# Head shifts of a unit turned in one group, local values by tokens, and query and key parts laid out by head

## What is computed

```python
k_c = k_pad.reshape(B, H, nb, G * D) @ Wck      # 32 blocks of 16 keys, compressed
out_c = softmax(where(c_ok, q @ k_c / scale, NEG)) @ v_c
_, top_idx = jax.lax.top_k(logits_c, 4)         # the 4 best blocks of each token
out_s = softmax over the keys of those blocks, where key <= token
wmask = (abs(pos[:, None] - pos[None, :]) <= 32) & (pos[:, None] >= pos[None, :])
out_l = softmax(where(wmask, q @ k / scale, NEG)) @ v
out = gates[..., 0:1] * merge(out_c) + gates[..., 1:2] * merge(out_s) + gates[..., 2:3] * merge(out_l)
return out @ Wo
```

## Time and profile before

| | |
|---|---|
| median of 3 runs | 1507.11 us (1507.01 to 1509.83) |
| the profiled execution | 1507.87 us, its span in the trace 1506.1 us |
| mean granted TensorE clock | 0.979 of full speed |
| TensorE busy | 1420.1 us, 94% of the span |
| VectorE / ScalarE / GpSimd busy | 1187.8 / 928.4 / 919.1 us |
| DMA | 113.74 MB, 76 GB/s over the span |

### The profile page before, as it was taken

The page is one execution under the profiler, slowest core; times in us unless marked ns, Lnnn a source line. Parts: engine busy times, 40 slices in busy tenths (PEclk is TensorE's granted clock), DMA queues, the critical chain, the costliest instruction groups (busy, mean ns, idle before and its releaser), DMA issues. The chain is left out here.

```text
span 1506.1 us, 43877 instructions
## 1 busy us (share of the span) xinstructions
PE 1420.1 (94%) x14960; PEld 1044.1 (69%) x14960; DVE 1187.8 (79%) x4544; ACT 928.4 (62%) x1684; POOL 919.1 (61%) x845
## 2 busy tenths in 40 slices
PE   6899679999999999999999999999999999999978
PEld 4566447777777777777777777777777777777657
DVE  5444288888888888888888888898888888888812
ACT  3766336666666666666666666666666666666641
POOL 4655356666666666666666666666666666666620
PEclk8999879999999999999999999999999999999989
DMA  6556942221111122222111122212222222222027
GB/s 186 205 183 211 274 73 53 52 51 45 47 45 47 50 51 51 51 51 50 47 46 46 47 50 49 48 48 51 51 51 51 51 51 51 65 51 53 9 95 234
DMA packets 217147, 113.74 MB, mean 76 GB/s; under 512 B 128872, under 2 KB 211224, under 8 KB 217112
## 3 DMA queue, kind: packets, MB, share of 16 engines
q1 hardware_dynamic: 216304, 112.88, 27.3%
q10 hardware_dynamic: 808, 0.42, 0.2%
HBM read 73.08 MB, written 40.16 MB: 75 GB/s over the span
## 5 line engine op out<-in xcount | busy, mean ns | idle before, releaser
L1150 POOL TENSOR_TENSOR sumxy<-xy 128x1024 f32<-128x1024 f32 x128 | 240.7, 1901 | 0.0
L1393 DVE TENSOR_REDUCE bmax<-q_bank 128x32 f32<-128x512 f32 (+3 forms) x512 | 219.9, 481 | 16.5 <-PE q_bank L1633 15.4
L1240 ACT ACTIVATE pts<-k_bank 128x512 f32<-128x512 f32 (+2 forms) x384 | 177.4, 490 | 42.0 <-PE k_bank L1668 41.2
L1494 DVE SCALAR_TENSOR_TENSOR mw<-sumxy,c,ex 128x1024 f32<-128x1024 f32 x128 | 176.0, 1394 | 1.5 <-issue 0.8
L1633 PE MATMUL q_bank<-ko,qo 96*128 96x512 bf16 (+3 forms) x512 | 142.9, 306 | 24.6 <-DVE bmax L1393 22.6
L1116 POOL TENSOR_TENSOR pad<-pad 128x1 f32<-128x1 f32 x32 | 6.2, 193 | 256.4 <-DVE top L1412 256.4
L1615 PE MATMUL f_bank<-xt,wfu 128*128 128x128 f32 x1024 | 162.3, 281 | 0.0
L1174 POOL TENSOR_TENSOR cw<-cw,mw 128x1024 f32<-128x1024 f32 x64 | 150.8, 2356 | 6.6 <-ACT mw L1264 1.6
L1615 PE MATMUL f_bank<-xt,wfg 128*128 128x128 f32 x1024 | 150.3, 279 | 0.0
L1615 PEld LDWEIGHTS f_bank<-xt,wfu 128*128 128x128 f32 x1024 | 139.4, 191 | 11.5
L1264 ACT ACTIVATE mw<-mw,erec 128x1024 f32<-128x1024 f32 x128 | 145.7, 1139 | 0.0
(11 more groups left out here) (211 smaller groups left out, 3340.1 us busy)
## 6 DMA issues: line engine op xcount, KB each, us to landing
qo<-s_qs SPq DMA_DIRECT2D x192, 64.0 KB, 2.2
ko<-s_ks SPq DMA_DIRECT2D x186, 64.0 KB, 2.2
s_qs<-parts SPq DMA_DIRECT2D x8, 768.0 KB, 4.7
s_ks<-parts SPq DMA_DIRECT2D x8, 768.0 KB, 6.3
s_v<-vo SPq DMA_DIRECT2D x8, 544.0 KB, 3.0
vv<-s_v SPq DMA_DIRECT2D x32, 136.0 KB, 2.3
vw<-s_v SPq DMA_DIRECT2D x64, 68.0 KB, 2.5
xin<-in_L_attn_x_dram SPq DMA_DIRECT2D x8, 512.0 KB, 6.9
```

The lines of the kernel that those rows point to most:

```text
L1150: done("sum_done", g_.tensor_tensor(sumxy[:, h, :, :], xy[:, 0, h, 0:XK, None].broadcast_to([P, XK, KEYS]), xy[:, 1, h, None, :].broadcast ...
L1240: last = s.activation(pts[:, h, OFFS[j]:OFFS[j] + n], bank[:, 0:n], ACT.Exp)
L1393: last = v.tensor_reduce(bmax[:, i, h, 0:n], Q.bank(job)[:, o:o + n * BLK].rearrange("p (n j) -> p n j", j=BLK), AX.X, ALU.max)
L1494: done("mw_done", v.scalar_tensor_tensor(mw[:, h, :], sumxy[:, h, :, :].rearrange("p a b -> p (a b)"), c8[:, h, 7:8], ex[:, h % 2, :], ALU ...
```

## The change

1. `qo` and `ko` are laid out by head. The six parts lie in three pairs, and the pair that would lie in a head's own quarter (rows 32h to 32h + 31 for head h) lies in the last quarter instead. The own quarter of head h holds the shifts of that head; the one of head 3 is the last. Until the shifts are there it holds zeros, loaded from a small DRAM tensor `s_zero` that the setup fills. So `queries` and `window` use all 128 rows. The loads become 20 DMAs for queries (4 of zeros) and 16 for keys, 36 in place of 12.
2. The shifts of the four heads are turned by one group of 4 products of 128 columns of weights, the first of the step, and ScalarE copies the four quarters one after the other ahead of its tanh (job a, first of ring K).
3. The local values are made by tokens: the exponentials are the weights, the values stream, and the result needs no turning back. The 64 products come in two halves on either side of `mlp_down(t, 3)`; a signal vl_half keeps the second from starting before the first is done. VectorE reads the bank directly; job tl, a copy on ScalarE and four transposes go.
4. `expert_sum` stands ahead of `key_marks`.
5. `yr` of batch 0 is loaded during the unit stage, and batch 1 waits for its `ar` alone before its transposes.
6. In the unit stage's lead, the block rows of `ko` come by 4 DMAs from ScalarE's queue in place of a copy on GpSimd. Some signals are merged into one with a count (strike_pc, xy_cand, e8_nmax).

```diff
-            SP3 = 96
+            PARTS = ((0, 0), (2, 0)), ((0, 1), (0, 2)), ((1, 0), (1, 1))
...
-            k_jobs = ["pcT", "co", "a0"]
+            k_jobs = ["a", "pcT", "co"]
             for h in range(HG):
-                k_jobs += [f"s{h}0", f"s{h}1", f"s{h}2"] + [f"a{h + 1}"] * (h < HG - 1) + [("pl0", "pl1", "vl", "tl")[h]]
-            k_jobs += ["vs", "ts"]
+                k_jobs += [f"s{h}0", f"s{h}1", f"s{h}2"] + [f"pl{h}"] * (h < 2)
+            k_jobs += ["vl", "vs", "ts"]
...
+            def part_rows(to, src, which, half):
+
+                for i, pair in enumerate(PARTS):
+                    lots = [(3, i, i + 1)] + [(i, h0, h1) for h0, h1 in ((0, i), (i + 1, HG)) if h0 < h1]
+                    for quad, h0, h1 in lots:
+                        for n in range(2):
+                            o = 32 * quad + D * n
+                            yield to[o:o + D, half, h0:h1, :], src[pair[n][which]][:, h0:h1, :]
...
-                    pairs = [(to[D * n:D * n + D, half, :, :], src[r])
-                             for to, src, parts in ((qo, q, Q_ROWS), (ko, k, K_ROWS))[:2 if keys else 1] for n, r in enumerate(parts)]
-                    send(pairs, parts_in[half], N_PARTS if keys else N_PARTS // 2)
+                    pairs = [(qo[32 * h:32 * h + 32, half, h, :], s_zero) for h in range(HG)]
+                    pairs += part_rows(qo, q, 0, half)
+                    if keys:
+                        pairs += part_rows(ko, k, 1, half)
+                    send(pairs, parts_in[half], N_PARTS if keys else N_QUERIES)
...
+                sp.dma_start(yr0[:, :, :], s_y[0:G].rearrange("i p c -> p i c")).then_inc(batch_in[0], 16)
...
-                for n, r in enumerate(K_ROWS):
-                    act.dma_start(ko[D * n:D * n + D, 0, :, :], k_first[r]).then_inc(parts_in[0], 16)
+                for h in range(HG):
+                    act.dma_start(ko[32 * h:32 * h + 32, :, h, :],
+                                  onehot[96:128, None, :].broadcast_to([32, 2, T])).then_inc(key_blocks, 16)
+                for dst, src in part_rows(ko, k_first, 1, 0):
+                    act.dma_start(dst, src).then_inc(parts_in[0], 16)
...
+                def head_shifts(t):
+
+                    K.wait_full(act, t, "a")
+                    for h in range(HG):
+                        rows = slice(32 * h, 32 * h + 32)
+                        last = s.activation(qo[rows, t.half, h, :], K.bank("a")[rows, :], ACT.Copy)
+                    K.released("a", last)
...
                 def step(t):
                     n = None if t.tail else t.next()
+                    head_shifts(t)
                     tanh(t, "w0", sw[:, 0:512], "tw_done")
...
+                    expert_sum(t)
+                    if n:
                         key_marks(n)
...
-                def local_values(t):
+                def local_values(t, r):
 
                     bank = K.bank("vl")
-                    for g in range(T // 32):
-                        for h in range(HG):
-                            rows, k = slice(64 * (h // 2), 64 * (h // 2) + 64), h % 2
-                            last = mm(bank[32 * h:32 * h + VW, 32 * g:32 * g + 32], vw[rows, t.half, g, VW * k:VW * k + VW],
-                                      pT[rows, k, 32 * g:32 * g + 32], start=True, stop=True, skip_group_check=True)
-                    K.filled("vl", last)
+                    rows = slice(64 * r, 64 * r + 64)
+                    for k in range(2):
+                        for g in range(T // 32):
+                            i, q = divmod(g, 4)
+                            o = VW * (HG * i + 2 * r + k)
+                            last = mm(bank[32 * q:32 * q + 32, o:o + VW], pT[rows, k, 32 * g:32 * g + 32],
+                                      vw[rows, t.half, g, VW * k:VW * k + VW], start=True, stop=True, skip_group_check=True)
+                    if r == 0:
+                        done("vl_half", last)
+                    else:
+                        K.filled("vl", last)
```

More of the change, by code:

```diff
@@ L273, in build @@
             b4 = sb("b4", [96, 2, 2, P], BF16)
+            zeros = sb("zeros", [32, T], BF16)
             bank = [ps(f"sbank{i}", [P, 512]) for i in range(4)]
@@ L299, in _ @@
                     sp.dma_start(dst, src).then_inc(to, 16)
-                sp.wait_ge(proj_in, 3 * 16)
+                sp.wait_ge(zeroed, 1)
+                sp.dma_start(s_zero, zeros[:, :]).then_inc(proj_in, 16)
+                sp.wait_ge(proj_in, 4 * 16)
             @block.gpsimd
@@ L311, in _ @@
                 g.memset(b1[:, :, :, :], 0.0).then_inc(cleared, 1)
+                g.memset(zeros[:, :], 0.0).then_inc(zeroed, 1)
                 for k, m in enumerate((ident, identb)):
@@ L879, in build @@
         projecting.close()
+        sb, _, _ = make(outer)
+        yr0 = sb("yr0", [P, TT, C])
         inner = ExitStack()
@@ L1338, in step @@
                     shifts_and_blocks(t)
-                    openings(t)
+                    tanh(t, "g0", hidden(0), "th_done")
                     share(t, 2)
@@ L1632, in queries @@
                         n = P * (i + 1)
-                        last = mm(bank[:, o:o + n], qo[0:SP3, t.half, h, P * i:P * i + P], ko[0:SP3, t.half, h, 0:n],
+                        last = mm(bank[:, o:o + n], qo[:, t.half, h, P * i:P * i + P], ko[:, t.half, h, 0:n],
                                   start=True, stop=(i > 0))
@@ L1651, in window @@
                                 o = 64 * (TT * h2 + i)
-                                k_ = (ko[0:SP3, t.half, h, s0 - 32:s0 + 32] if s0 else
-                                      ko[0:SP3, t.half, h, 0:32][:, None, :].broadcast_to([SP3, 2, 32]))
-                                last = mm(bank[32 * q:32 * q + 32, o:o + 64], qo[0:SP3, t.half, h, s0:s0 + 32], k_,
+                                k_ = (ko[:, t.half, h, s0 - 32:s0 + 32] if s0 else
+                                      ko[:, t.half, h, 0:32][:, None, :].broadcast_to([P, 2, 32]))
+                                last = mm(bank[32 * q:32 * q + 32, o:o + 64], qo[:, t.half, h, s0:s0 + 32], k_,
                                           start=False, stop=True, skip_group_check=True)
@@ L1659, in keys_rows @@
                 def keys_rows(t, h, part):
-                    if part == 0:
-                        K.wait_read(pe, t, f"a{h}")
+                    if (h, part) == (0, 0):
+                        K.wait_read(pe, t, "a")
                     job = f"s{h}{part}"
@@ L1763, in mlp_down @@
                     for f in (2 * part, 2 * part + 1):
+                        if f == FT - 1:
+                            need(pe, "vl_half", t)
                         mm(Y.bank("y")[:, 0:C], hT[:, f, :], wfd[:, f, :], start=(f == 0), stop=False)
@@ L1845, in build @@
             ar = [ar0] + [sb(f"ar{b}", [P, TT, C]) for b in range(1, B)]
-            yr = [sb(f"yr{b}", [P, TT, C]) for b in range(B)]
+            yr = [yr0] + [sb(f"yr{b}", [P, TT, C]) for b in range(1, B)]
             aT = sb("aT", [P, 2, 2, T])
@@ L1891, in transposed @@
                 def transposed(n):
[L1892 removed]
+                    pe.wait_ge(batch_in[n.index], 32 if n.index == 1 else 48)
                     for c in range(2):
@@ L1936, in step @@
                 def step(t, n):
-                    dve.wait_ge(batch_in[t.index], 48)
+                    if t.index == 1:
+                        dve.wait_ge(yr1_in, 16)
+                    else:
+                        dve.wait_ge(batch_in[t.index], 48)
                     for j in range(2):
```

129 lines of the change are left out of this document (55 added, 74 removed).

## The result

The changed kernel takes 1524.23 us (median of 4 runs, 1523.74 to 1526.22) against 1508.47 us for the kernel before on the same chip: a ratio of 1.0104 (95% interval 1.0086 to 1.0122). It is slower by 1%, where 1490 was forecast. The profiled execution is 1523.74 us, its span 1521.9, 15.8 more than before.

What follows compares the result with a forecast made beforehand. TensorE bounds the kernel, neck and neck with VectorE; 1507.9 less 16 (30 steps), 0.8 and 1.4, plus 4.7 (lead), less 3.0 (final loads) is 1491.4, against the median 1490.6, forecast 1490. Range 1465 to 1510.

Steps and rivals of the forecast that it cites:

- Behind it nothing holds TensorE: From the query p21 to the next step's start: no waits, 16.8 us less one group (0.33) and transposes (0.44), 16.0.
- p21: TensorE's query of head 2, part 2, the forecast's mark within a step; at 742.19 us in the kernel before.
- E to p21: From a step's first TensorE product (E) to the query p21: 22.11 us before, 22.38 forecast, as VectorE waits for ScalarE's exponential.
- The early sum: Sum of shares ahead of key marks: GpSimd's candidates start some 2.7 us sooner, VectorE's stretched addition (1.20 us) is relieved.
- TensorE's own stream: TensorE's work in a step falls by 1.43 us (shift groups 1.04, transposes 0.44, split 0.05), which would allow 37.5.
- rival 2: At each step's start the shifts come late and the group waits 0.4 us: 1502 us, chance 0.13.
- M: The moment in a step when the second window bank is full (714.81 us before), 5.27 us ahead of E.
- rival 4: Local values on TensorE lose their overlap: nearly 300 us at most, 37 us at 20 ns a record; chance 0.03.
- rival 3: SP's 36 load issues become the bound, at the wait for parts_in: 1550 us at a 0.58 pitch; chance 0.10.
- Rival 1: TensorE keeps all it saves in each step: step 37.5 us, 1463 us in all, chance 0.20.
- Once only: Outside the repeated steps: the lead costs 4.7 us (ScalarE's 20 DMAs, w0 at low clock), the final loads save 3.0.
- The sum again: Whole span: 16 us less in 30 steps, 0.8 at step 0's end, 1.4 in the last, +4.7 lead, -3.0 final loads.

Runs made afterwards that it cites:

- up_first: The changed kernel with VectorE's up(t, 1) moved ahead of unselected and best_pairs: 1497.85 us, ratio 0.9919.
- cover_back: The changed kernel with the first half of the local values moved back ahead of mlp_down part 2: 1496.98 us, ratio 0.9917.
- shifts_by_head: up_first with the shift edit undone (groups, copies, loads and block rows of ko as before): 1491.77 us, ratio 0.9885.
- before_sum_early: The kernel before with only the sum of shares moved ahead of key_marks: 1498.41 us, ratio 0.9928.
- up_first_sum_back: up_first with the sum of shares put back behind the maxima of head 2: 1540.35 us, ratio 1.0203.
- w0_first: up_first with TensorE's w0 ahead of the transposed shifts, ScalarE's copies behind its last exponential, share(t, 1) behind g0's tanh: 1474.78 us.
- sum_back: The changed kernel with the sum of shares put back behind the maxima of head 2: 1539.90 us, ratio 1.0200.
- marks_late: up_first with key_marks moved from ahead of gate(t, 1) to behind up(t, 1): 1620.31 us, ratio 1.0714.

## Why the prediction was wrong, step by step

**The step that failed: "Behind it nothing holds TensorE", 16.0 us from p21 to the next step.** The sum of the subtraction (16.8 less a group and the transposes) came out as TensorE's own work: up_first and cover_back measure 15.91. Its two terms did not, and that they nearly cancel is luck: the group was worth 0.75 and not 0.33, the local values without transposes 0.14 and not 0.44 (16.80 before, 16.66 in shifts_by_head). The changed kernel has 16.73, because the local values were counted as work that is moved at no cost, and not as the cover of up(t, 1). 0.82 us in 31 steps is 25 of the 34 us by which the forecast missed. The text asked of each engine what it waits for ahead of p21, and never of VectorE's product behind it.

**E to p21: 22.38 forecast, 22.62 measured.** The mechanism was right (the third masked product waits for the exponential; the waits for the maxima grew to 70.8 us), the size short. The four copies took 2.38 us, 0.6 each, where I took the 0.5 of full copies, so that product starts at E + 5.05 and not E + 4.76. 0.24 x 31 is 7 us more.

**The early sum.** I named the relief of VectorE's addition (0.68 us now, 1.20 before) but credited it to the shifts alone. By itself the early sum is worth 10 us (before_sum_early), 0.32 a step ahead of p21: the shift edit's true loss there is 0.83 (22.62 against 21.79), where I had 0.27. Two errors of opposite sign made the 22.38 look near.

**TensorE's own stream: 1.43 less.** Its busy time fell by 1.8 a step, so the work did go; no run has a step without waits, so the 37.5 itself was not measured.

**The shifts at the start (rival 2).** GpSimd ends the shifts at 732.16, M + 4.81, where I had 4.8; M to E is 5.27 us again (727.35 to 732.62) and no wait is recorded in the steps: right, and up_first_sum_back shows that it hangs on the early sum.

**Local values (rival 4).** 64 records take 0.66 us, 1.36 in all: right. The loads (rival 3): 36 issues from 719.54 to 737.01, 0.485 each, and no wait for them in the steps: right. Rival 1 fell with VectorE's waits.

**Once only.** The lead cost 6.8 us and not 4.7 (p21 of step 0 at 242.95, before at 236.14): ScalarE's 20 issues end at 196.8 and not 194.9, and w0 at the low clock took 3.73 us (granted clock 0.50 from 200 to 215, 0.58 from 215 to 225). Of the 6.8, 3.9 lie behind the lead's last query (28.07 us from there to p21, now 32.02). The rest is known only roughly, since that query falls anywhere from 209.4 (w0_first) to 215.2 (sum_back) in the runs whose code up to there is the same. The wait for the final load fell from 6.5 to 2.8, by 3.7 and not 3.0. ScalarE in the lead:

```profile
186.01 2.70 ACTq L1248 DMA_DIRECT2D ko<-onehot  x4
188.74 8.07 ACTq L1251 DMA_DIRECT2D ko<-s_ks  x16
196.94 0.60 ACT L1295 ACTIVATE sim<-f_bank 128x512 f32<-128x512 f32 x1 [26.43 <-issue]
```

**The sum again:** the end of step 0 comes 7.3 us later (260.12, before 252.82), the 30 steps behind it take 12.85 more in all (0.43 each), and from there to the end of the span it takes 4.35 less, 3.7 of it the final load: 15.8, as much as the span grew.

No rival named this place. The one on the slower side that I gave most to, the loads, looked at the resource whose count the diff tripled; the loss came from an instruction whose text the diff doesn't touch.

## What to carry to other kernels

When work is moved, ask of every wait that it stood in front of: what was it covering, and is the awaited result early enough without it? Where an engine is near the bound, a moved cover can cost more than the wait that the profile then shows (0.82 us for 0.56 here). And try the pieces apart: here one small piece held a gain of 0.7%, and four moves of a line or two turned the whole from 1.0% slower to 2.3% faster.

## What the runs showed of the hardware

- VectorE's unselected, one input and one output in SBUF, took 0.41 to 0.42 us where it began ahead of GpSimd's next large addition, 1.37 when it began 0.82 us behind GpSimd's addition and 1.96 when it began 0.23 us behind it: each time it ends with the first of GpSimd's two additions, some 0.2 us behind its end. MAX8, right behind it and beside the second addition, kept 0.15 us each. The Trainium skill (SBUF — State Buffer, "SBUF: two separate sides") says that the port pair that VectorE and GpSimd share is an exclusive lock for the whole instruction, which GpSimd's instructions take, and VectorE's in a 2-port perf mode or with two inputs in SBUF. That VectorE's instruction ends only behind GpSimd's agrees with a lock; which mode it ran in no trace shows.
- ScalarE's copy of 32 partitions by 512 (float32 to bf16) took 0.59 us, as long as one of 128 partitions by 512 (float32, 0.59 to 0.60): a quarter of the partitions saved nothing. Four in a row kept a pitch of 0.6, where two of the large ones took 1.09 us together.
- A wait of 0.56 us on TensorE, by its record, cost 0.82 us of the step; a group of 0.33 us (start to start) cost 0.75. The records of pipelined products tell less than the distance between fixed points.
- In marks_late the granted clock fell to 0.50 behind a wait of 2.29 us, and 32 records of products that took 2.35 us at full clock took 4.15.
- Local values on one row group, 64 records in 0.66 us, kept the pace of 10 ns each (128 in 1.38 before). The Trainium skill (TensorE: Matmul & The Clock Gate, Part 3) has weight loads overlap only where the row group differs; this run doesn't show the loss that would follow.
